# The last layer of a fused four-layer kernel: shared expert's down products per unit, tokens of two blocks turned ahead, scatter from the first choice's slots

## The reference, cut to what matters

```python
T = x.shape[0]                                  # 1024 tokens, h = 256
logits = x @ router_w                           # 8 experts
top_logits, top_indices = jax.lax.top_k(logits, 2)
scores = jax.nn.softmax(top_logits, axis=-1)
...
for e in range(E):                              # INTER = 512
    f1 = permuted * mask @ w1[e]                # 256 x 1024
    g, u = jnp.split(f1, 2, axis=-1)
    act = jax.nn.silu(g) * u
    out = out + jnp.where(mask, act @ w2[e], 0.0)   # 512 x 256
...
combined = (unperm.reshape(T, TOPK, h) * scores[..., None]).sum(axis=1)
shared = jax.nn.silu(x @ w_gate) * (x @ w_up) @ w_down   # 256 x 1024, 1024 x 256
return (combined + shared).reshape(b, s, h)
```

## Time and profile before

| | us |
|---|---|
| median of 3 runs | 1105.83 (1105.2 to 1108.23) |
| profiled execution | 1113.83 |
| its span | 1112.1 |
| PE busy, share of the span | 919.5 (83%) |
| DVE busy | 620.2 (56%) |
| ACT busy | 526.3 (47%) |
| POOL busy | 252.4 (23%) |
| last feed-forward part, first logits matmul to end | 859.9 to 1112.1 |

### The profile page before, as it was taken

How to read it: one execution, slowest core, us unless ns; L and a number is a source line. 1 busy time by engine, 2 the same in 40 slices (tenths; PEclk the granted TensorE clock), 3 DMA queues, 4 the chain that set the end, 5 groups by cost and what they waited for, 6 DMA issues and landing times. The chain is left out here.

```text
span 1112.1 us, 15443 instructions
## 1 busy us (share of the span) xinstructions
PE 919.5 (83%) x5390; PEld 539.1 (48%) x5416; DVE 620.2 (56%) x1304; ACT 526.3 (47%) x794; POOL 252.4 (23%) x297
## 2 busy tenths in 40 slices
PE   5698987998998548799799467787866978999996
PEld 2244435666487324444357423333435454666654
DVE  4577755445345875745456579999985411111123
ACT  3166664222423665578643169898982102222210
POOL 4010100000000001313542127667771230000031
PEclk9599999899899869999899765655567899999999
DMA  3613301000357004667144547878650021111022
GB/s 123 155 35 74 110 15 47 1 1 1 127 65 80 0 1 121 184 162 129 44 189 83 196 86 150 162 150 185 108 91 13 24 71 29 41 45 48 24 59 70
DMA packets 130445, 91.64 MB, mean 82 GB/s; under 512 B 92805, under 2 KB 119631, under 8 KB 128591
## 3 DMA queue, kind: packets, MB, share of 16 engines
q1 hardware_dynamic: 125522, 83.45, 33.4%
q0 software_dynamic: 1536, 4.20, 1.2%
q10 hardware_dynamic: 3312, 3.02, 0.8%
HBM read 56.09 MB, written 15.86 MB: 65 GB/s over the span
## 5 line engine op out<-in xcount | busy, mean ns | idle before, releaser
L2270 ACT ACTIVATE sb_l_E<-PS,sb_l_NB,sb_L3SQS 128x1024 uint8<-128x1024 f32 x128 | 154.4, 1207 | 22.7 <-DVE sb_l_NB L2304 13.0
L2301 DVE TENSOR_REDUCE sb_l_NM<-PS 128x1 f32<-128x1024 f32 x128 | 155.5, 1215 | 5.3 <-PE PS L2244 5.3
L2244 PE MATMUL PS<-sb_l_K,sb_l_Q 128*128 128x512 bf16 x232 | 115.4, 589 | 40.9 <-ACT sb_l_E L2270 33.1
L2209 POOL CAST sb_l_ET<-sb_l_EP 128x1024 bf16<-128x1024 uint8 x128 | 128.5, 1040 | 79.0 <-DMA sb_l_EP<-sb_l_E 77.3
L613 DVE TENSOR_REDUCE sb_negmax<-PS 128x2 f32<-128x512 f32 x128 | 84.1, 690 | 31.6 <-PE PS L463 31.4
L2254 PEld LDWEIGHTS PS<-sb_L3VI,sb_l_ET 128*128 128x128 bf16 x1024 | 54.8, 112 | 72.5 <-issue 46.8
L1368 PE MATMUL PS<-sb_L3w,sb_block_xT 128*128 x184 | 83.0, 594 | 4.5 <-DVE sb_hidden L1458 3.0
L599 ACT ACTIVATE sb_E<-PS 128x1024 f32<-128x1024 f32 x64 | 65.4, 1023 | 42.2 <-PE PS L526 42.2
L923 ACT ACTIVATE sb_E<-PS 128x1024 f32<-128x1024 f32 x64 | 65.3, 1024 | 24.6 <-PE PS L830 20.9
L463 PE MATMUL PS<-sb_K,sb_Q 96*128 96x256 bf16 x256 | 53.9, 302 | 15.9 <-ACT sb_negmax_T L573 10.3
L1458 DVE TENSOR_TENSOR sb_hidden<-sb_hidden,PS 128x512 f32<-128x512 f32 x23 | 15.8, 688 | 88.2 <-ACT sb_hidden L1423 88.2
(11 more groups left out here) (336 smaller groups left out, 1720.9 us busy)
## 6 DMA issues: line engine op xcount, KB each, us to landing
sb_Q<-q SPq DMA_DIRECT2D x48, 192.0 KB
sb_L3w<-L3w SPq DMA_DIRECT2D x16, 512.0 KB, 6.7
sb_K<-k SPq DMA_DIRECT2D x24, 192.0 KB
sb_W2E<-L3w SPq DMA_DIRECT2D x8, 512.0 KB, 4.7
q<-sb_q_parts SPq DMA_DIRECT2D x12, 256.0 KB, 4.0
xs<-zero_row SPq DMA_DIRECT2D x1, 2944.0 KB, 47.9
sb_block_x<-xs SPq DMA_DIRECT2D x23, 128.0 KB, 2.2
ys<-sb_block_y ACTq DMA_DIRECT2D x23, 128.0 KB, 2.4
```

The source lines that it names most:

```text
L2209: return eng.tensor_copy(ET[:, u % CRING], EP[:, u // 2 % TRING, :, :, u % 2])
L2244: ins = pe.matmul(core.bank(2 * (n % SRING) + half), Q[:, h % RING, t * P:(t + 1) * P], K[:, h % RING, half * HALF:(half + 1) * HALF], sta ...
L2270: act.activation(E[:, n // 2 % ERING, :, n % 2], S(n), ACT.Exp, bias=NB[:, n:n + 1], scale=scale_of(h, t), accum_out=ZS[:, n:n + 1]).then_ ...
L2301: dve.tensor_reduce(NM[:, n:n + 1], S(n), axis=AX.X, op=ALU.max, negate=True).then_inc(maxed, 1)
```

## The change

The shared down product no longer runs tile by tile at the end of a half. After each shared unit, PE adds that unit's share to all four token tiles (`shared_part`), which stand open in two PSUM banks, two tiles to a bank: banks 6 and 7 in the first half, 6 and 4 in the second. Only the two hidden slices in work are kept. DVE adds each bank to the residual in one instruction (`add_shared`); in the second half after all merges. Tiles 0 to 3 are merged in step 37 and tiles 4 to 7 in step 38. The tokens of blocks 0 and 1 are turned after the last part of the first half, and those of block b+2 in the step of block b. POOL starts the scatter with all tiles of the first choice as soon as the first choice's slots stand (`placed`), and goes on with the second choice.

```diff
-            chain(dve.tensor_copy(SLOT[k][:, :], SF[:, :]))
+            dve.tensor_copy(SLOT[k][:, :], SF[:, :]).then_inc(placed, 1)
+            dve.wait_ge(placed, k + 1)
...
-    downs_at = [[] for n in range(NU + 2)]
...
+    shared_index = lambda n: n if n < SC else n - BLOCKS
+    SHARED_BANKS = ((6, 7), (6, 4))
...
-    HS = core.sb(ctx, "shared_hidden_T", [P, SC, HALF], F32)
+    HS = core.sb(ctx, "shared_hidden_T", [P, 2, HALF], F32)
...
-            pool.wait_ge(routed, 1)
             pool.wait_ge(core.xs_cleared, 16)
-            for t in range(NT):
-                for k in range(2):
+            for k in range(2):
+                pool.wait_ge(placed, k + 1)
+                for t in range(NT):
                     pool.indirect_dma_start(xs, bass.IndirectOffsetOnAxis(ap=SLOT[k][:, t:t + 1], axis=0),
                                             core.XN[:, t, :], None).then_inc(scattered, 16)
...
-                sp.wait_ge(merged, 2 * (t + 1))
+                if t < NT // 2:
+                    sp.wait_ge(merged, 2 * (t + 1))
+                else:
+                    sp.wait_ge(x_added, t // 2 + 1)
...
             def turn_hidden(b):
...
+                if b == 1:
+                    pe.wait_ge(x_added, 2)
...
+            def go_down(b):
+                if b == 0:
+                    pe.wait_ge(x_added, 2)
                 else:
+                    pe.wait_ge(y_out, b)
+                pe.wait_ge(h_out, b + 1)
...
+            def shared_part(n):
+                kind, half, k = units[n]
+                pe.wait_ge(hidden, n + 1)
+                if half and k == 0:
+                    pe.wait_ge(h_out, BLOCKS)
+                    pe.wait_ge(x_out, BLOCKS)
+                for t in range(4):
+                    ins = pe.matmul(core.PS[:, SHARED_BANKS[half][t // 2], t % 2 * D:(t % 2 + 1) * D],
+                                    HS[:, k % 2, t * P:(t + 1) * P], WD[:, k, :], start=(k == 0 and t % 2 == 0), stop=(k == SC - 1 and t % 2 == 1))
+                    ins.then_inc(shared_down, 1)
...
-            for n in range(NU + 2):
+            for n in range(NU + 1):
                 if n < NU:
                     go_up(n)
                 if n == 1:
                     pe_counts(pe)
+                if n >= 1 and units[n - 1][0] == "shared" and n != SC:
+                    shared_part(n - 1)
+                if n == SC - 1:
+                    shared_part(n)
+                    turn_x(0)
+                    turn_x(1)
+                if n >= 1 and units[n - 1][0] == "block":
                     turn_hidden(units[n - 1][2])
+                if n < NU and units[n][0] == "block" and units[n][2] + 2 < BLOCKS:
+                    turn_x(units[n][2] + 2)
+                if 2 <= n and units[n - 2][0] == "block":
+                    go_down(units[n - 2][2])
...
+                    if kind == "shared" and shared_index(n) >= 2:
+                        act.wait_ge(shared_down, 4 * (shared_index(n) - 1))
...
+                if n == SC - 1:
+                    for b in range(2):
+                        copy_x(b)
+                if n < NU and units[n][0] == "block" and units[n][2] + 2 < BLOCKS:
+                    copy_x(units[n][2] + 2)
...
+            def add_shared(half, pair):
+                dve.wait_ge(shared_down, 4 * SC * (half + 1) - 2 + 2 * pair)
+                X = core.X[:, 4 * half + 2 * pair:4 * half + 2 * pair + 2, :].rearrange("p t d -> p (t d)")
+                if half:
+                    dve.wait_ge(merged, 2 * NT)
+                dve.tensor_tensor(X, X, core.bank(SHARED_BANKS[half][pair]), ALU.add).then_inc(x_added, 1)
...
+                if n == NU - 2:
+                    dve.wait_ge(x_added, 2)
                     for t in range(4):
                         merge(t)
+                if n == NU - 1:
+                    for t in range(4, NT):
+                        merge(t)
+            for pair in range(2):
+                add_shared(1, pair)
```

More of the change, by code:

```diff
@@ L1317, in _ @@
                 pool.wait_ge(y_stored[r], 16 * ((BLOCKS - 1 - r) // YRING + 1))
-            pool.wait_ge(down, down_count[("block", BLOCKS - 1)])
+            pool.wait_ge(down, BLOCKS)
             for t in range(NT):
@@ L1378, in turn_hidden @@
                 ins.then_inc(h_turned, 1)
[L1380 to L1387, removed]
-                else:
[L1389 to L1392, removed]
-                ins.then_inc(down, 1)
+            def go_down(b):
+                if b == 0:
+                    pe.wait_ge(x_added, 2)
+                else:
+                    pe.wait_ge(y_out, b)
+                pe.wait_ge(h_out, b + 1)
+                for k in range(HC):
+                    w = core.W2E[:, bass.ds(expert[b], 1), k * D:(k + 1) * D].rearrange("p e n -> p (e n)")
+                    ins = pe.matmul(core.PS[:, 7, 0:D], HT[:, b % 2, k, :], w, start=(k == 0), stop=(k == HC - 1))
+                ins.then_inc(down, 1)
+            def shared_part(n):
[8 more added lines that the diff above has]
+                    ins.then_inc(shared_down, 1)
             pe_logits(pe)
-            for n in range(NU + 2):
+            for n in range(NU + 1):
                 if n < NU:
@@ L1400, in _, with copy_x @@
                     pe_counts(pe)
[L1401 to L1410 removed]
+                if n >= 1 and units[n - 1][0] == "shared" and n != SC:
[5 more added lines that the diff above has]
+                if n >= 1 and units[n - 1][0] == "block":
+                    turn_hidden(units[n - 1][2])
+                if n < NU and units[n][0] == "block" and units[n][2] + 2 < BLOCKS:
+                    turn_x(units[n][2] + 2)
+                if 2 <= n and units[n - 2][0] == "block":
+                    go_down(units[n - 2][2])
         @block.scalar
         def _(act):
+            def copy_x(b):
+                act.wait_ge(x_turned, b + 1)
+                if b >= 2:
+                    act.wait_ge(up, block_unit(b - 2) + 1)
+                act.activation(XBT[:, b % 2].rearrange("p c n -> p (c n)"), core.PS[:, 4, 0:D], ACT.Copy
+                               ).then_inc(x_out, 1)
             act_route(act)
@@ L1434, in _ @@
                     if b >= 2:
-                        act.wait_ge(down, down_count[("block", b - 2)])
+                        act.wait_ge(down, b - 1)
                     act.activation(HT[:, b % 2].rearrange("p k n -> p (k n)"), core.bank(5 + b % 2), ACT.Copy
@@ L1460, in _ @@
+            dve_choose(dve)
+            for n in range(NU):
+                dve.wait_ge(silued, n + 1)
+                dve.tensor_tensor(hidden_of(n), hidden_of(n), core.bank(2 * (n % 2) + 1), ALU.mult
+                                  ).then_inc(hidden, 1)
                 if n == 1:
                     dve_place(dve)
-                for kind, i in downs_at[n]:
-                    dve.wait_ge(down, down_count[(kind, i)])
-                    if kind == "block":
-                        if i >= YRING:
-                            dve.wait_ge(y_stored[i % YRING], 16 * (i // YRING))
-                        dve.tensor_copy(YB[:, i % YRING, :], core.PS[:, 7, 0:D]).then_inc(y_out, 1)
-                    else:
-                        dve.tensor_tensor(core.X[:, i, :], core.X[:, i, :], core.PS[:, 7, 0:D], ALU.add
-                                          ).then_inc(y_out, 1)
-                        dve.wait_ge(y_out, down_count[(kind, i)])
-                        if i >= 4:
-                            merge(i)
@@ L1474, in _ @@
-                if n == NU - SC + 7:
+                if n == SC - 1:
+                    for pair in range(2):
+                        add_shared(0, pair)
+                if n >= 2 and units[n - 2][0] == "block":
+                    b = units[n - 2][2]
+                    dve.wait_ge(down, b + 1)
+                    if b >= YRING:
+                        dve.wait_ge(y_stored[b % YRING], 16 * (b // YRING))
+                    dve.tensor_copy(YB[:, b % YRING, :], core.PS[:, 7, 0:D]).then_inc(y_out, 1)
```

37 lines of the change are left out of this document (8 added, 29 removed).

## The result

The changed kernel takes 1098.02 us (median of 6 runs, 1093.11 to 1102.12) beside 1106.29 for the kernel before in the same runs: ratio 0.9913, 95% interval 0.9892 to 0.9934.

What follows compares the result with a forecast made beforehand. PE was taken as full in the expert blocks, with stalls and slow clock at the last layer's ends. Gains 10.3 + 3.6 + 0.2 + 6.3 = 20.4 us off the median 1105.83 gave 1085.4, range 1082.5 to 1092.

Steps and rivals of the forecast that it cites:

- the last of the sum: Final step: the gain inside the last layer of one profiled execution, subtracted from the median 1105.83, gives 1085.4 us.
- The 20.4: Total forecast gain in us in the last layer: 10.3 + 3.6 + 0.2 + 6.3.
- part 1: First half of the shared expert to block 0's start: PE stalls, drains and slow clock go, gain 10.3 us.
- the unnamed 3.3: Unexplained 3.3 us within PE's 3.77 us stall in the first half's shared down product, counted as removed.
- the slow tile's 1.7: Slow clock in the first half's second shared down tile (5.42 against 3.72), counted as 1.7 us removed.
- part 3: Second half's shared units to the end: DVE ends last, gain 7.1 us, net 6.3 after the last stores.
- Part 2: Tokens turned two blocks ahead: PE stalls before blocks 1 and 2 go, gain 3.6 us.
- The unnamed wait: Unexplained DVE wait before first shared adds, taken as gone; rival: stays before last adds, 1088.7, chance 0.18 with register load.
- the gone stall behind the placing: PE's 0.96 us stall at 882.27, from DVE's placing chain ahead of unit 2's product, was to vanish.
- no wait for the gather at the merges: At the end, gathered rows land at T + 41, needed at T + 45.9, T being the second half's first unit.
- Its cover: Time between block 0's tokens landing and PE reaching them, said to grow from 2.8 to 6.0 us.
- The rule: Skill page: increments on packed matmuls cost 26.3 ns each; 8 to 64 would lose up to 1.5 us, giving 1086.9.

Runs made afterwards that it cites:

- before_again: The kernel before, unedited, timed and profiled again: 1108.88 us, beside 1107.47 for the same kernel.
- after_again: The changed kernel, unedited, timed and profiled again: 1097.25 us, beside 1107.47 for the kernel before.
- late_scatter: The changed kernel with the scatter as before (tile by tile, both choices, after the whole placing): 1101.11 us, beside 1114.91 for the kernel before.
- scatter_delayed: The changed kernel with the scatter held back until the product of shared unit 4: 1110.07 us, beside 1114.91 for the kernel before.
- after_third: The changed kernel, unedited, in a later set of runs: 1100.69 us, beside 1115.84 for the kernel before.
- best2: The changed kernel with merges spread, block 0's tokens turned earlier, last block's down product and store first: 1095.16 us, beside 1115.84 for the kernel before.
- best: The changed kernel with merges spread and block 0's tokens turned between the first half's last two shared parts: 1096.04 us, beside 1114.91 for the kernel before.
- before_third: The kernel before, unedited, in a later set of runs: 1115.10 us, beside 1115.84 for the same kernel.
- scatter_only: The kernel before with only the scatter begun at the first choice's slots: 1112.48 us, beside 1115.84 for the kernel before.
- merge_early: The changed kernel with merges spread, tiles 0 to 5 earlier, only 6 and 7 after the last product: 1094.96 us, beside 1114.91 for the kernel before.

## Why the prediction was wrong

**The step that failed is the last of the sum**: "the gain is a difference inside one layer, so I subtract it from the median". The 20.4 was a difference to one execution, whose part held 9.85 us more than that of before_again (252.20 against 242.35), and by their times the executions of the median were of the second kind. Two terms are mis-sized by it. In part 1 the gain of 10.3 contains the unnamed 3.3 and the slow tile's 1.7; to block 0 the profiles without waits give 56.12 - 50.88 = 5.2. In part 3, forecast at 6.3, the gain is 6.6 in the first pair of profiles (57.88 to 51.30) and 1.7 without the wait (52.98 to 51.26). Part 2's 3.6 plus 0.2 measured 3.7 (189.37 - 56.12 less 180.45 - 50.88). Sum 10.6, and 20.4 less 9.85 is 10.6. It lies within the intervals of the first result (8.3; 7.3 to 11.9 from its ratio) and of after_again (10.2; 7.1 to 11.0). The hint was on the table: an execution 8.0 us above a median that spreads over 3 us, and two waits in it that no row named.

**The rivals looked at the wrong side.** The unnamed wait was asked about only in the changed kernel, as a risk of 3.3 us. That it might be missing in the median of before, and so be no gain at all, was no rival, and by the times it was the case. The prediction also put the second half's late start at 3.1 to 3.3; from the end of PE's tile (1087.24 + 3.69 = 1090.93) to 1093.96 it is 3.03, and 3.20 is DVE's whole idle.

**Right, point by point.** The pace of the parts (1.73), the gone stall behind the placing, block 0 at 50.8 (50.7), no idle before blocks 1 and 2, the block period 5.82, no wait for the gather at the merges, the merges' end 1.6 us past PE's and the span's end 231.7 after the part's start (231.8). Clock 1.00 from 882 to 915 (the old slow tile ran at a granted clock of 0.68, behind an idle of 3.77 us). That the early scatter is worth nothing by itself: late_scatter, to 0.01 us at block 0. Its cover is 5.2 (6.0 forecast), by scatter_delayed.

**The rule weighed.** A cost of 26.3 ns per increment ("TensorE: Matmul & The Clock Gate", "The cost: per-tile semaphore tail", Trainium skill), given there for packed tiles, would have added up to 1.5 us, an estimate from that page. The two parts with eight increments take 3.45, twice a block's down of 1.73 with one, and DVE's add starts 0.04 us behind them (913.28 after 913.24): the trace doesn't agree that they cost anything here.

**Wrong beside that**: the unnamed wait was expected to be gone in the changed kernel "since the adds now fall after the gather's and the scatter's last transfer". The adds of the second half are free of it, but where it occurs in the changed kernel it stands ahead of ACT's Silu, one unit earlier (late_scatter, after_third: 3.5 to 3.7 us of T to end). The first profile of the changed kernel came without it, so here the forecast came true without its reason being tested.

## What to carry to other kernels

Before a sum made on one profiled execution is subtracted from a median, account for the difference between the two: look in that profile for waits that no row names, and price the change with and without them. A wait that is there in one set of runs and not in another made this change worth 10 us in one and 15 in the other, so both kernels have to be timed together, and a gain found on one chip should be measured on a second. Slack behind the place of such a wait is worth something as well: with the wait, the earlier gather of best2 took 1.9 us off T to end against best.

## What the hardware showed that was not expected

In nine executions an engine's instruction that waited for PE started late for no reason in the rows, 19 times in all. Due is the end of PE's work, or the last start plus the period of 5.16; the last column counts from the start of POOL's last indirect issue.

| kernel, half | engine | due | started | last issue | started after it |
|---|---|---|---|---|---|
| before, first | DVE | 901.40 | 904.69 | 901.14 | 3.55 |
| before, second | DVE | 1090.93 | 1093.96 | 1090.06 | 3.90 |
| before_third, first | DVE | 908.62 | 910.99 | 908.35 | 2.64 |
| before_third, second | DVE | 1095.49 | 1098.26 | 1094.61 | 3.65 |
| scatter_only, first | DVE | 903.30 | 904.19 | 900.75 | 3.44 |
| scatter_only, second | DVE | 1088.69 | 1091.52 | 1087.81 | 3.71 |
| late_scatter, first | ACT | 900.9 | 903.06 | 902.39 | 0.67 |
| late_scatter, second | ACT | 1077.7 | 1082.40 | 1078.51 | 3.89 |
| scatter_delayed, first | DVE | 909.2 | 913.17 | 912.49 | 0.68 |
| scatter_delayed, first, next add | DVE | 913.9 | 916.02 | 912.49 | 3.53 |
| scatter_delayed, second | ACT | 1088.3 | 1092.90 | 1089.02 | 3.88 |
| merge_early, first | ACT | 900.4 | 902.66 | 898.94 | 3.72 |
| merge_early, second | ACT | 1077.2 | 1081.83 | 1078.18 | 3.65 |
| best, first | ACT | 909.4 | 911.58 | 907.99 | 3.59 |
| best, second | ACT | 1084.5 | 1089.18 | 1085.46 | 3.72 |
| after_third, first | ACT | 904.4 | 906.41 | 902.94 | 3.47 |
| after_third, second | ACT | 1081.2 | 1085.58 | 1081.94 | 3.64 |
| best2, first | ACT | 903.4 | 905.51 | 901.96 | 3.55 |
| best2, second | ACT | 1073.4 | 1076.84 | 1074.57 | 2.27 |

The lateness runs from 0.9 to 4.7 us, but 17 of the 19 starts stand at 2.3 to 3.9 after the last issue's start, on either engine, and two at 0.7. That points to the end of the indirect transfers without showing it, since the places in the program lie close together too. Slower transfers don't explain it: in the three us behind the scatter's last issue the DMA engines are busy alike in before and before_again (half us by half us 0.53, 0.21, 0.00, 0.73, 0.00, 0.00 in both), and in late_scatter they stand still from 1081.10 on, 1.3 us ahead of the Silu. What releases the wait, and why three sets of runs have none of it and two have it in every profile, stays open; the kernels made to tell ran in sets without it.

After PE's idle of 3.25 to 3.77 us ahead of the second down tile that tile took 5.28 to 6.57 us, at a granted clock of 0.56 to 0.70; after 2.84 (before_third, first half) it took 3.72, at 1.00. For a part of such a tile the windows show the clock at 0.50, the lower of its two levels (1.2 of 2.4 GHz): in before from 907 to 909 and from 1094.44 to 1097.40, in before_third from 1098.74 to 1104.
